# A shared expert beside a mixture's combination: four batches at a time in high and low parts, and one batch moved to it from the routing stage

## The chip, the cores and the metric

One core of one Trainium2 chip runs the whole program in one launch. The metric is the device time in microseconds (us); below it is that of the only core. The kernel before was run three times: 3481.93, 3479.44 and 3477.32 us, median 3479.44 us.

## The reference

Two decoder layers on 2048 tokens of width 512, each of self attention, cross attention and a mixture of experts, each with a residual and a layer norm. The change lies in the first layer's mixture. It has 32 routed experts of width 256 with four chosen per token and at most 80 rows each, and one shared expert of width 512 that every token passes:

```
topk_idx, topk_w = _router(x, router_w, e_bias)
...
Y = einsum('eci,eid->ecd', silu(G) * U, W_down)
out = zeros(T, d).at[slots_token].add(Yf)
shared = silu(x @ shared_gate.T) * (x @ shared_up.T) @ shared_down.T
return out + shared
```

Then `x = layernorm(x + ffn(x))`. All values are fp32.

## The kernel before

The program is written by hand as stages, each a block in which the five engines run their own instruction lists, with semaphores between them and a barrier at the end. The tokens are held as 16 batches of 128 in `moe_xall`. Three stages matter here.

*Late routing* (`late_routing`, names `cd_`). VectorE finishes the routing of the last two pairs of batches, GpSimd sends the tokens' rows to `packed`, SP loads the weights of the first eight experts (`load_first`), and TensorE fills its time with the shared expert of the first `EARLY` = 5 batches (`SharedExpert`).

*Routed experts* (`capped_experts`, `m_`). 32 experts in turn, TensorE against a ring of eight weight slots. The results go to `result` in memory. Rows of `moe_base` that hold nothing yet are borrowed as buffers.

*Combination* (`combine`, `cc_`). For every batch GpSimd gathers the four chosen rows per token (`gather`, four indirect DMAs of 256 KB, four batches ahead), VectorE adds them with their weights to `moe_base` (four L2561), takes mean and variance (L2569, L2572), GpSimd the inverse root (`norm`), and VectorE normalises into `cc_yn` (L2577), which SP stores to `x2`. Beside it the other 11 batches pass the shared expert.

`SharedExpert` works a batch at a time on unsplit fp32 operands. `turn_x` transposes the batch's tokens (L1536), ScalarE copies them out (`cc_sxT`), `up` makes the gate and the up product (L1543): for each of 4 blocks of the width, 4 products of a 128x128 weight with 128 tokens. ScalarE takes the SiLU, VectorE multiplies (`hidden`, L1525), `down` makes 4 products with 512 columns (L1564), and `add` puts the result onto `moe_base` (L1530). Each fp32 product appears in the trace as two records on TensorE. The order on TensorE is written out in `tensor`:

```
pe.wait_ge(self.act_g, done(k - 1))
self.up(pe, self.pG, self.wg, k, self.pe_g)
if k == 1:
    pe.wait_ge(self.wd_in, 16)
down(k - 1)
pe.wait_ge(self.v_h, done(k - 1))
self.up(pe, self.pU, self.wu, k, self.pe_u)
```

The shared weights lie in `all_staged`, three slots of 1 MB. When the last products have used them, ScalarE loads the next attention's three weights there (`ahead`).

## Time and profile before

| | |
|---|---|
| median of three runs | 3479.44 us |
| the profiled execution | 3482.6 us |
| its span, first to last instruction | 3480.8 us |
| mean granted TensorE clock | 0.955 |
| TensorE matmuls busy | 3159.6 us (91%) |
| VectorE busy | 2094.4 us (60%) |
| ScalarE busy | 1278.2 us (37%) |
| GpSimd busy | 1450.4 us (42%) |

The profiled execution is one execution of the same program, 3 us above the median. Busy is the time in which an engine worked on an instruction; an engine can be busy and yet not be the one that the others wait for. A row of the time line gives start, duration, engine, line, output and inputs, and in brackets how long the engine had been idle and what released it. "issue" stands where the profile shows nothing that was waited for.

### The profile page before, as it was taken

How to read it: one execution, taken by the hardware profiler on the slowest of the kernel's cores; microseconds unless marked ns; L12 is line 12 of the kernel's file. 1: busy time of each engine (PE TensorE's matmuls, PEld its weight loads, DVE VectorE, ACT ScalarE, POOL GpSimd, SP SyncE). 2: the span in 40 equal slices, each digit the busy share in tenths (PEclk: the TensorE clock that was granted, in tenths of full speed). 3: DMA queues.
4: the chain of work that ended last, by engine and by line, in shares of the span. 5: the costliest groups of instructions: out<-in, count | busy, mean ns of one | idle time of the engine just before them, and what ended most of it. 6: DMA issues, size and time to landing. Idle time of an engine off the chain costs nothing. (4 is left out here: it accounts for less than half of the span.)

```text
span 3480.8 us, 58860 instructions
## 1 busy us (share of the span) xinstructions
PE 3159.6 (91%) x21152; PEld 2638.6 (76%) x21152; DVE 2094.4 (60%) x3767; ACT 1278.2 (37%) x3276; POOL 1450.4 (42%) x1470
## 2 busy tenths in 40 slices
PE   7999999999969999799896999699999999869991
PEld 6887878878847777678685777488888888758881
DVE  5666566576645776421064777556667678645656
ACT  3333333333346666201102333244444444324430
POOL 4454343344422434300153222355555556544445
PEclk9999999999989999789998999799999999979996
DMA  4001016022310111339563112211101001156665
GB/s 172 18 16 51 0 35 232 0 95 102 141 33 24 53 32 57 144 100 340 171 143 115 37 42 63 99 56 34 36 12 47 12 24 43 39 199 223 225 221 157
DMA packets 137872, 317.18 MB, mean 91 GB/s; under 512 B 18425, under 2 KB 30457, under 8 KB 135538
## 3 DMA queue, kind: packets, MB, share of 16 engines
q1 hardware_dynamic: 120194, 274.61, 23.4%
q0 software_dynamic: 15360, 36.25, 3.9%
q10 hardware_dynamic: 2160, 4.21, 0.4%
q8 instruction: 99, 1.62, 0.2%
q14 instruction: 59, 0.48, 0.0%
HBM read 231.07 MB, written 98.04 MB: 95 GB/s over the span
## 5 line engine op out<-in xcount | busy, mean ns | idle before, releaser
L398 POOL TENSOR_TENSOR a_sq<-a_tq,a_sinq 128x256 f32<-128x256 f32 x128 | 150.3, 1194 | 358.4 <-DVE a_tq L474 358.4
L398 POOL TENSOR_TENSOR a_sk<-a_tk,a_sink 128x256 f32<-128x256 f32 x128 | 123.8, 986 | 90.0 <-DVE a_tk L474 90.0
L364 ACT COPY a_probT<-bank 128x512 f32<-128x512 f32 x64 | 37.6, 587 | 328.3 <-PE bank L713 328.3
L411 POOL TENSOR_TENSOR e_sk<-e_tk 128x512 f32<-128x512 f32 x64 | 66.6, 1040 | 204.6 <-DVE e_tk L501 204.6
L353 ACT ACTIVATE e_prob<-bank,e_nb,e_rq 128x128 f32<-128x128 f32 x256 | 113.9, 455 | 86.7 <-DVE e_nb L575 86.7
L348 ACT ACTIVATE a_sm<-a_sm,a_nmax 128x128 f32<-128x128 f32 x256 | 99.8, 391 | 121.7 <-DVE a_nmax L570 121.7
L952 ACT ACTIVATE b_prob<-bank,b_nb 128x128 f32<-128x128 f32 x512 | 139.4, 387 | 11.6 <-DVE b_nb L1148 11.3
L1046 POOL TENSOR_TENSOR d_prob<-d_prob,d_nmax 128x1024 f32<-128x1024 f32 x32 | 64.0, 1999 | 183.3 <-DVE d_nmax L1143 183.3
L2340 POOL TENSOR_TENSOR n_wu_lo<-nw_wu,n_wu_hi 128x1408 fp32r<-128x1408 f32 x23 | 74.0, 3218 | 135.4 <-DVE n_wu_hi L2384 135.4
L496 DVE TENSOR_TENSOR a_kr<-a_kr,a_sk 128x512 f32<-128x512 f32 x64 | 66.4, 1037 | 89.0 <-POOL a_sk L398 89.0
L1145 DVE TENSOR_REDUCE b_nmax<-bank 128x8 f32<-128x1024 f32 x64 | 77.9, 1217 | 68.6 <-PE bank L1289 67.9
L81 PE MATMUL bank<-a_wq_hi,a_x_lo 128*128 128x512 f32 x256 | 107.7, 421 | 7.1 <-DVE a_wq_lo L214 7.0
L943 ACT COPY b_probT<-bank 128x512 f32<-128x512 f32 x128 | 78.5, 613 | 90.5 <-PE bank L1298 90.5
L81 PE MATMUL bank<-e_wo_hi,e_z_lo 128*128 128x512 f32 x256 | 107.5, 420 | 3.1 <-DVE e_z_lo L538 3.1
L81 PE MATMUL bank<-a_wo_hi,a_z_lo 128*128 128x512 f32 x256 | 105.8, 413 | 2.9 <-DVE a_z_lo L538 2.9
L413 POOL TENSOR_TENSOR e_sq<-e_tq 128x512 f32<-128x512 f32 x64 | 66.7, 1042 | 96.3 <-DVE e_tq L505 96.3
L386 POOL TENSOR_TENSOR a_x_lo<-a_xall,a_x_hi 128x512 fp32r<-128x512 f32 x64 | 89.6, 1400 | 41.2 <-ACT a_x_hi L320 41.2
L81 PE MATMUL bank<-a_wk_hi,a_x_lo 128*128 128x512 f32 x256 | 100.7, 393 | 5.2 <-DVE a_wk_lo L214 5.1
L364 ACT COPY e_probT<-bank 128x512 f32<-128x512 f32 x64 | 37.6, 587 | 179.7 <-PE bank L713 179.7
L2345 POOL TENSOR_TENSOR n_wd_lo<-nw_wd,n_wd_hi 128x1024 fp32r<-128x1024 f32 (+1 forms) x46 | 85.8, 1885 | 39.4 <-ACT n_wd_hi L2313 39.4
L572 DVE TENSOR_REDUCE e_nmax<-bank 128x4 f32<-128x512 f32 x64 | 44.2, 690 | 96.0 <-PE bank L697 96.0
L83 PE MATMUL bank<-e_wo_hi,e_z_hi 128*128 128x512 f32 x256 | 102.0, 398 | 0.0
(512 smaller groups left out, 10718.8 us busy)
## 6 DMA issues: line engine op xcount, KB each, us to landing
packed<-all_zero SPq DMA_DIRECT2D x32, 1024.0 KB, 8.3
cw_wg<-in_c_wg SPq DMA_DIRECT2D x32, 512.0 KB
cw_wu<-in_c_wu SPq DMA_DIRECT2D x32, 512.0 KB
cw_wd<-in_c_wd SPq DMA_DIRECT2D x32, 512.0 KB
nw_wg<-in_f_wg SPq DMA_DIRECT2D x23, 704.0 KB
nw_wu<-in_f_wu SPq DMA_DIRECT2D x23, 704.0 KB
nw_wd<-in_f_wd SPq DMA_DIRECT2D x23, 512.0 KB
nw_xe<-packed SPq DMA_DIRECT2D x46, 256.0 KB, 2.7
```

Source lines behind the costliest of these rows:

```text
L81: nc.tensor.matmul(ps, a_lo, b_hi, start=start, stop=False)
L83: return nc.tensor.matmul(ps, a_hi, b_hi, start=False, stop=stop)
L348: step = nc.scalar.activation(prob[:, j, :], sm[:, j, :], ACT.Exp, bias=nmax[:, j:j + 1], accum_out=rsum[:, j:j + 1])
L353: step = nc.scalar.activation(prob[:, j, :], pS[:, P * j:P * j + P], ACT.Exp, bias=nb[:, j:j + 1], scale=rq[:, par, j:j + 1], accum_out=rs ...
L364: nc.scalar.copy(probT[:], pP[:, :]).then_inc(act_pt, 1)
L386: sub = nc.gpsimd.tensor_tensor(x_lo[:, par].rearrange("p c t -> p (c t)"), xall[:, b, :], x_hi[:, par].rearrange("p c t -> p (c t)").bitc ...
L398: step = nc.gpsimd.tensor_tensor(o, i, s, ALU.mult)
L943: nc.scalar.copy(probT[:, s // 2 % 2, s % 2], pP[:, :]).then_inc(act_pt, 1)
L952: step = nc.scalar.activation(prob[:, p % 2, i], pS[:, i // H, P * (i % H):P * (i % H) + P], ACT.Exp, bias=nb[:, p % 2, i:i + 1], scale=SCALE)
L1145: nc.vector.tensor_reduce(nmax[:, p], scores, AX.X, ALU.max, negate=True).then_inc(v_nm, 1)
L2340: nc.gpsimd.tensor_tensor(lo["u"][:, w], raw["u"][:, w], hi["u"][:, w].bitcast(F32), ALU.subtract).then_inc(g_u, 1)
L2345: sub = nc.gpsimd.tensor_tensor(o, x, y.bitcast(F32), ALU.subtract)
```

## The change

`EARLY` goes from 5 to 4, and the other 12 batches pass a new class, `SharedQuads`, in the combination: three groups of four batches. Each of the three weights and the tokens are split into a high part (a copy of type fp32r on ScalarE) and a low part (the difference, on VectorE), and each product becomes three: low by high, high by low, high by high (`split_product`, which the attentions use already). With four batches side by side a weight block stays in place for 512 columns. The hidden values are split too. Eight banks are used in pairs. The tile `cc_yn` goes, the normalised batch is written over its sum, and the gathered rows of three of the four slots go over the raw shared weights once their low parts exist. VectorE's combinations are placed by hand between the steps of a group; the last four batches have their gathered rows summed first and the shared part added last. The loads of the next attention's weights wait for the sums that read those slots.

On TensorE the start of the combination stood so (`cc_sxT` tokens, `all_staged` weights, `cc_gate` hidden values):

```order
L1536 MATMUL bank<-all_ident,moe_xall 128x128 x8
L1543 MATMUL bank<-cc_sxT,all_staged 128x128 x32
L1536 MATMUL bank<-all_ident,moe_xall 128x128 x4
L1543 MATMUL bank<-cc_sxT,all_staged 128x128 x16
L1564 MATMUL bank<-all_staged,cc_gate 128x512 x4
L1543 MATMUL bank<-cc_sxT,all_staged 128x128 x16
L1536 MATMUL bank<-all_ident,moe_xall 128x128 x4
L1543 MATMUL bank<-cc_sxT,all_staged 128x128 x16
```

Now four batches are turned first, and then every product is a triple. The first rows:

```order
L1675 MATMUL bank<-all_ident,moe_xall 128x128 x16
L81 MATMUL bank<-cc_sx_hi,cc_wg_lo 128x512
L82 MATMUL bank<-cc_sx_lo,cc_wg_hi 128x512
L83 MATMUL bank<-cc_sx_hi,cc_wg_hi 128x512
```

and the start of the down phase of the first group:

```order
L1675 MATMUL bank<-all_ident,moe_xall 128x128 x4
L81 MATMUL bank<-cc_wd_hi,cc_h_lo 128x512
L82 MATMUL bank<-cc_wd_lo,cc_h_hi 128x512
L83 MATMUL bank<-cc_wd_hi,cc_h_hi 128x512
```

Four transposes of a batch to come now stand ahead of each batch's down triples, and no down product stands between the gate and the up products.

On VectorE a batch in the middle stood so:

```order
L1525 TENSOR_TENSOR cc_gate<-cc_gate,bank 128x512
L1530 TENSOR_TENSOR moe_base<-bank,moe_xall 128x512
L2561 SCALAR_TENSOR_TENSOR cc_acc<-cc_got,moe_weight,moe_base 128x512
L2561 SCALAR_TENSOR_TENSOR cc_acc<-cc_got,moe_weight,cc_acc 128x512 x3
L2569 BN_STATS cc_stats<-cc_acc 128x6
L70 MEMSET cc_still 128x1
L2572 BN_AGGR cc_mv<-cc_stats 128x2
L2577 TENSOR_SCALAR cc_yn<-cc_acc,cc_mv,cc_rstd 128x512
```

Now, one quarter of the up phase of a group:

```order
L1661 TENSOR_TENSOR cc_gate<-cc_gate,bank 128x512
L1666 TENSOR_TENSOR cc_h_lo<-cc_gate,cc_h_hi 128x512
L2706 SCALAR_TENSOR_TENSOR cc_acc<-all_staged,moe_weight,moe_base 128x512
L2706 SCALAR_TENSOR_TENSOR cc_acc<-all_staged,moe_weight,cc_acc 128x512 x3
L2711 BN_STATS cc_stats<-cc_acc 128x6
L70 MEMSET cc_still 128x1
L2714 BN_AGGR cc_mv<-cc_stats 128x2
L2722 TENSOR_SCALAR cc_acc<-cc_acc,cc_mv,cc_rstd 128x512
```

The base add has left this place and stands in the down phase; the low part of the hidden values has come in.

The end of VectorE's list was, from the last batch's sums on:

```order
L2561 SCALAR_TENSOR_TENSOR cc_acc<-cc_got,moe_weight,moe_xall 128x512
L2561 SCALAR_TENSOR_TENSOR cc_acc<-cc_got,moe_weight,cc_acc 128x512 x3
L2567 TENSOR_TENSOR cc_acc<-bank,cc_acc 128x512
L2569 BN_STATS cc_stats<-cc_acc 128x6
L70 MEMSET cc_still 128x1
L2572 BN_AGGR cc_mv<-cc_stats 128x2
L2577 TENSOR_SCALAR cc_yn<-cc_acc,cc_mv,cc_rstd 128x512 x2
```

and the first part of the end is now:

```order
L2706 SCALAR_TENSOR_TENSOR cc_acc<-cc_got,moe_weight,moe_xall 128x512
L2706 SCALAR_TENSOR_TENSOR cc_acc<-cc_got,moe_weight,cc_acc 128x512 x3
L2706 SCALAR_TENSOR_TENSOR cc_acc<-all_staged,moe_weight,moe_xall 128x512
L2706 SCALAR_TENSOR_TENSOR cc_acc<-all_staged,moe_weight,cc_acc 128x512 x3
L1670 TENSOR_TENSOR cc_acc<-bank,cc_acc 128x512
L2711 BN_STATS cc_stats<-cc_acc 128x6
L70 MEMSET cc_still 128x1
L2714 BN_AGGR cc_mv<-cc_stats 128x2
L2722 TENSOR_SCALAR cc_acc<-cc_acc,cc_mv,cc_rstd 128x512
L2706 SCALAR_TENSOR_TENSOR cc_acc<-all_staged,moe_weight,moe_xall 128x512
L2706 SCALAR_TENSOR_TENSOR cc_acc<-all_staged,moe_weight,cc_acc 128x512 x3
L1670 TENSOR_TENSOR cc_acc<-bank,cc_acc 128x512
```

Before, one batch had its shared part added last; now the last four have, with their sums and statistics behind the last group's hidden values.

The diff, cut to its core:

```diff
+class SharedQuads:
+    QUAD = 4
...
+        self.pX, self.pG, self.pU, self.pO = (banks[:, 2 * n:2 * n + 2, :] for n in range(4))
+        self.raw, self.raw_in = [staged.tile[:, n] for n in range(3)], staged.parts
...
+    def weight_hi(self, act, n):
+        act.wait_ge(self.raw_in[n], 16)
+        self.nc.scalar.copy(self.hi[n][:], self.raw[n]).then_inc(self.w_hi[n], 1)
+    def take_x_hi(self, act, n):
+        act.wait_ge(self.pe_x, done(n))
+        if n >= self.QUAD:
+            act.wait_ge(self.pe_u, done(C * (n // self.QUAD) - 1))
+        self.nc.scalar.copy(self.x_hi[:, :, self.columns(n)], self.pX[:, n % 2].rearrange("p (c t) -> p c t", c=C)).then_inc(self.act_x, 1)
+    def scalar(self, act):
+        self.take_x_hi(act, 0)
+        self.weight_hi(act, 0)
+        for n in range(1, Q):
+            self.take_x_hi(act, n)
+        self.weight_hi(act, 1)
+        self.weight_hi(act, 2)
+        for q in range(self.quads):
+            for f in range(C):
+                k = C * q + f
+                act.wait_ge(self.pe_g, done(k))
+                act.wait_ge(self.v_hl, done(k - 2))
+                nc.scalar.activation(self.gate[:, f % 2], self.pG[:, f % 2], ACT.Silu).then_inc(self.act_g, 1)
+                act.wait_ge(self.v_h, done(k))
+                act.wait_ge(self.pe_o, done(Q * q - 1))
+                nc.scalar.copy(self.h_hi[:, f], self.h[:, f % 2]).then_inc(self.act_h, 1)
+            if q < self.quads - 1:
+                for j in range(Q):
+                    self.take_x_hi(act, Q * (q + 1) + j)
+    def weight_lo(self, dve, n):
+        dve.wait_ge(self.w_hi[n], 1)
+        self.nc.vector.tensor_tensor(self.lo[n][:], self.raw[n], self.hi[n][:].bitcast(F32), ALU.subtract).then_inc(self.w_lo[n], 1)
+    def take_x_lo(self, dve, n):
+        dve.wait_ge(self.act_x, done(n))
+        own = self.columns(n)
+        self.nc.vector.tensor_tensor(self.x_lo[:, :, own], self.pX[:, n % 2].rearrange("p (c t) -> p c t", c=C),
+                                     self.x_hi[:, :, own].bitcast(F32), ALU.subtract).then_inc(self.v_x, 1)
+    def begin_vector(self, dve):
+        self.take_x_lo(dve, 0)
+        self.weight_lo(dve, 0)
+        for n in range(1, self.QUAD):
+            self.take_x_lo(dve, n)
+        self.weight_lo(dve, 1)
+    def hidden(self, dve, k):
+        f = k % C
+        dve.wait_ge(self.act_g, done(k))
+        dve.wait_ge(self.pe_u, done(k))
+        self.nc.vector.tensor_tensor(self.h[:, f % 2], self.gate[:, f % 2], self.pU[:, f % 2], ALU.mult).then_inc(self.v_h, 1)
+    def hidden_lo(self, dve, k):
+        f = k % C
+        dve.wait_ge(self.act_h, done(k))
+        self.nc.vector.tensor_tensor(self.h_lo[:, f], self.h[:, f % 2], self.h_hi[:, f].bitcast(F32), ALU.subtract).then_inc(self.v_hl, 1)
...
+    def turn_x(self, pe, n):
+        pe.wait_ge(self.v_x, done(n - 2))
+        for c in range(C):
+            last = self.nc.tensor.transpose(self.pX[:, n % 2, P * c:P * c + P], self.xall[:, self.first + n, P * c:P * c + P], self.ident[:])
+        last.then_inc(self.pe_x, 1)
+    def up(self, ps, w, f, sem):
+        own = slice(P * f, P * f + P)
+        for c in range(C):
+            last = split_product(self.nc, ps[:, f % 2], self.hi[w][:, c, own], self.lo[w][:, c, own], self.x_hi[:, c, :], self.x_lo[:, c, :],
+                                 start=c == 0, stop=c == C - 1)
+        last.then_inc(sem, 1)
+    def down(self, pe, n):
+        q, own = n // self.QUAD, self.columns(n)
+        pe.wait_ge(self.v_b, done(n - 2))
+        for f in range(C):
+            pe.wait_ge(self.v_hl, done(C * q + f))
+            last = split_product(self.nc, self.pO[:, n % 2], self.h_hi[:, f, own], self.h_lo[:, f, own], self.hi[2][:, f, :], self.lo[2][:, f, :],
+                                 start=f == 0, stop=f == C - 1)
+        last.then_inc(self.pe_o, 1)
+    def tensor(self, pe):
+        for n in range(Q):
+            self.turn_x(pe, n)
+        for q in range(self.quads):
+            pe.wait_ge(self.v_x, done(Q * q + Q - 1))
+            for f in range(C):
+                k = C * q + f
+                if k == 0:
+                    pe.wait_ge(self.w_lo[0], 1)
+                pe.wait_ge(self.act_g, done(k - 2))
+                self.up(self.pG, 0, f, self.pe_g)
+                if k == 0:
+                    pe.wait_ge(self.w_lo[1], 1)
+                pe.wait_ge(self.v_h, done(k - 2))
+                self.up(self.pU, 1, f, self.pe_u)
+            if q == 0:
+                pe.wait_ge(self.w_lo[2], 1)
+            for j in range(Q):
+                if q < self.quads - 1:
+                    self.turn_x(pe, Q * (q + 1) + j)
+                self.down(pe, Q * q + j)
...
-        got = st.sbuf("got", [P, R, K, D])
+        own = st.sbuf("got", [P, 1 if shared else R, K, D])
-        yn = st.sbuf("yn", [P, R, D])
...
+        def got(n):
+            return own[:, n] if n == 0 or not shared else part.raw[n - 1]
...
-                for n, used in (("q", part.pe_g), ("k", part.pe_u), ("v", part.pe_o)):
-                    act.wait_ge(used, done(part.COUNT - 1))
+                for n, b in (("q", B - 3), ("k", B - 2), ("v", B - 1)):
+                    act.wait_ge(v_k, done(K * b + K - 1))
                     ahead(act, n)
...
-                sp.dma_start(x_dst[R * i + n], yn[:, n, :]).then_inc(y_out[n], 16)
+                sp.dma_start(x_dst[R * i + n], acc[:, n, :]).then_inc(y_out[n], 16)
...
-                pool.wait_ge(v_acc, done(b - R))
+                if shared and 0 < b < R:
+                    pool.wait_ge(part.w_lo[n - 1], 1)
+                if b >= R:
+                    pool.wait_ge(v_k, done(K * (b - R) + K - 1))
                 for k in range(K):
-                    nc.gpsimd.indirect_dma_start(got[:, n, k, :], None, result,
+                    nc.gpsimd.indirect_dma_start(got(n)[:, k, :], None, result,
...
+            def gathered(i, n, first):
                 b = R * i + n
                 dve.wait_ge(g_in[n], 16 * K * (i + 1))
-                dve.wait_ge(v_yn, done(b - R))
+                dve.wait_ge(y_out[n], landed(i))
                 for k in range(K):
                     if k:
-                        dve.wait_ge(v_k, done((K - 1) * b + k - 1))
-                    prev = acc[:, n] if k else part.xall[:, b] if shared_last else base[:, b]
...
+                        dve.wait_ge(v_k, done(K * b + k - 1))
+                    prev = acc[:, n] if k else first[:, b]
+                    nc.vector.scalar_tensor_tensor(out=acc[:, n], in0=got(n)[:, k, :], scalar=weight[:, b, k:k + 1], in1=prev,
+                                                   op0=ALU.mult, op1=ALU.add).then_inc(v_k, 1)
+                dve.wait_ge(v_k, done(K * b + K - 1))
+            def moments(b, n):
...
-                dve.wait_ge(y_out[n], landed(i))
-                nc.vector.tensor_scalar(yn[:, n], acc[:, n], mv[:, n, 0:1], rstd[:, n:n + 1], ALU.subtract, ALU.mult).then_inc(v_yn, 1)
+                nc.vector.tensor_scalar(acc[:, n], acc[:, n], mv[:, n, 0:1], rstd[:, n:n + 1], ALU.subtract, ALU.mult).then_inc(v_yn, 1)
+            def shared_last(b):
+                n, s = b % R, b - part.first
+                part.add(dve, s, acc[:, n], acc[:, n])
+                dve.wait_ge(part.v_b, done(s))
+                moments(b, n)
+                normed((b - 1) // R, (b - 1) % R)
             if shared:
-                head_start(dve, part.v_h, part.v_b)
+                Q, first, last = part.QUAD, part.first, part.quads - 1
+                part.begin_vector(dve)
                 b = 0
-                for k in range(part.COUNT + 1):
-                    if k < part.COUNT:
-                        part.hidden(dve, k)
-                    if 0 < k < part.COUNT:
-                        part.add(dve, k - 1)
-                    until = min(part.first + k, (k + 1) * B // part.COUNT, B)
-                    while b < until:
-                        if part.first <= b < B - 1:
-                            dve.wait_ge(part.v_b, done(b - part.first))
-                        tile(b // R, b % R, shared_last=b == B - 1)
-                        if b:
-                            normed((b - 1) // R, (b - 1) % R)
+                for q in range(part.quads):
+                    for f in range(C):
+                        part.hidden(dve, C * q + f)
+                        if q == 0 and f == 0:
+                            part.weight_lo(dve, 2)
+                        if f:
+                            part.hidden_lo(dve, C * q + f - 1)
+                        if f == C - 1:
+                            part.hidden_lo(dve, C * q + f)
+                        if b < first + Q * q:
+                            whole(b)
+                            b += 1
+                    if q < last:
+                        for j in range(Q):
+                            s = Q * q + j
+                            part.take_x_lo(dve, s + Q)
+                            part.add(dve, s, base[:, first + s, :], part.xall[:, first + s, :])
+                        dve.wait_ge(part.v_b, done(Q * q + Q - 1))
+                        whole(b)
                         b += 1
+                for c in (b, b + 1):
+                    gathered(c // R, c % R, part.xall)
+                for c in range(b, B):
+                    shared_last(c)
+                    if c + 2 < B:
+                        gathered((c + 2) // R, (c + 2) % R, part.xall)
                 normed(B // R - 1, R - 1)
                 return
...
-            EARLY = 5
-
-            def some(first, count):
-                return lambda st: SharedExpert(nc, st, psum, ident, xall, staged_c, base, first, count)
+            EARLY, QUADS = 4, 3
+            def early(st):
+                return SharedExpert(nc, st, psum, ident, xall, staged_c, base, 0, EARLY)
+            def rest(st):
+                return SharedQuads(nc, st, banks, ident, xall, staged_c, base, EARLY, QUADS)
...
                 weights = CappedWeights(Stage(nc, routed, "cw"), w)
-                late_routing(nc, "cd", psum, router, weight, some(0, EARLY), weights.load_first)
+                late_routing(nc, "cd", psum, router, weight, early, weights.load_first)
                 capped_experts(nc, psum, ident, packed1.rearrange("(e r) d -> e r d", r=80), result1, zero, weights,
                                base[0:80, B - weights.R:B], base[0:80, EARLY:EARLY + 2])
-            combine(nc, "cc", base, result1, router.rows, weight, x2, 4, some(EARLY, B - EARLY), staged_d.fetch)
+            combine(nc, "cc", base, result1, router.rows, weight, x2, 4, rest, staged_d.fetch)
```

## Rows read from the trace of the kernel before

**Rows 1.** Busy time by stage: late routing, experts, combination (engine busy us, records; TensorE clock).
```profile
1447.70:1521.60 73.90, 68.08 (x424) 56.98 (x424) 26.16 (x77) 8.23 (x15) 19.57 (x20) 0.89 0.46 172
1521.60:1717.90 196.30, 188.21 (x1280) 150.46 (x1280) 26.03 (x64) 28.36 (x64) 0.00 (x0) 0.94 0.73 246
1717.90:1864.90 147.00, 129.50 (x836) 106.47 (x836) 82.47 (x150) 11.92 (x22) 81.55 (x98) 0.93 0.65 162
```
**Rows 2.** Time line of TensorE in the combination (start us, duration us, engine, line, records).
```profile
1750.03 3.73 PE L1543 MATMUL bank<-cc_sxT,all_staged 128*128 128x128 f32 x32
...
1757.61 3.60 PE L1564 MATMUL bank<-all_staged,cc_gate 128*128 128x512 f32 x8
...
1761.05 3.73 PE L1543 MATMUL bank<-cc_sxT,all_staged 128*128 128x128 f32 x32
```
**Rows 3.** Time line of VectorE, one batch of the combination.
```profile
1764.89 0.69 DVE L1525 TENSOR_TENSOR cc_gate<-cc_gate,bank 128x512 f32<-128x512 f32 x1 [5.31 <-PE bank L1543]
1765.49 0.68 DVE L1530 TENSOR_TENSOR moe_base<-bank,moe_xall 128x512 f32<-128x512 f32 x1
1766.09 0.74 DVE L2561 SCALAR_TENSOR_TENSOR cc_acc<-cc_got,moe_weight,moe_base 128x512 f32<-128x512 f32 x1
...
1769.23 0.69 DVE L2569 BATCH_NORM_STATS2 cc_stats<-cc_acc 128x6 f32<-128x512 f32 x1
...
1770.06 0.53 DVE L2577 TENSOR_SCALAR cc_yn<-cc_acc,cc_mv,cc_rstd 128x512 f32<-128x512 f32 x1
...
1770.51 0.75 DVE L2561 SCALAR_TENSOR_TENSOR cc_acc<-cc_got,moe_weight,moe_base 128x512 f32<-128x512 f32 x1
```
**Rows 4.** Busy time by stretch, start of the combination (columns as in Rows 1).
```profile
1720.00:1726.00 6.00, 5.71 (x27) 5.74 (x28) 0.00 (x0) 0.15 (x1) 4.65 (x5) 0.50 0.68 182
1726.00:1730.00 4.00, 4.00 (x37) 4.00 (x36) 0.00 (x0) 1.07 (x2) 2.95 (x4) 0.99 0.75 215
1730.00:1742.00 12.00, 4.56 (x23) 3.42 (x22) 0.23 (x1) 0.00 (x0) 6.64 (x7) 0.76 0.65 188
```
**Rows 5.** Late routing: down products of two batches; then busy time of two stretches.
```profile
1497.81 3.67 PE L1564 MATMUL bank<-all_staged,cd_gate 128*128 128x512 f32 x8
...
1508.46 3.60 PE L1564 MATMUL bank<-all_staged,cd_gate 128*128 128x512 f32 x8
...
1450.00:1480.00 30.00, 27.07 (x168) 24.71 (x168) 9.15 (x42) 4.90 (x9) 15.39 (x16) 0.78 1.03 393
1480.00:1521.00 41.00, 38.74 (x250) 30.20 (x248) 14.53 (x26) 2.74 (x5) 2.93 (x3) 1.00 0.04 14
```
**Rows 6.** Time line, start of the next attention: copies, differences, products of parts.
```profile
1876.45 1.90 ACT L924 CAST d_wq_hi<-all_staged 128x2048 fp32r<-128x2048 f32 x1
...
1878.39 2.29 DVE L1106 TENSOR_TENSOR d_wq_lo<-all_staged,d_wq_hi 128x2048 fp32r<-128x2048 f32 x1 [1.11 <-ACT d_wq_hi L924]
...
1881.33 0.63 PE L1246 MATMUL bank<-d_wq_lo,d_x_hi 128*128 128x512 f32 x1
...
1885.59 0.63 PE L1246 MATMUL bank<-d_wq_hi,d_x_hi 128*128 128x512 f32 x1
...
1886.95 0.39 PE L1246 MATMUL bank<-d_wk_hi,d_x_lo 128*128 128x512 f32 x1
...
1889.44 0.39 PE L1246 MATMUL bank<-d_wv_hi,d_x_hi 128*128 128x512 f32 x1
```
**Rows 7.** Time line of GpSimd in the combination, gathers.
```profile
1771.87 1.04 POOL L2532 DMA_INDIRECT cc_got<-result,moe_rows  x1 [0.18 <-issue]
1773.22 1.23 POOL L2532 DMA_INDIRECT cc_got<-result,moe_rows  x1 [0.30 <-issue]
...
1778.14 0.99 POOL L2532 DMA_INDIRECT cc_got<-result,moe_rows  x1 [0.18 <-issue]
...
1832.43 1.33 POOL L2532 DMA_INDIRECT cc_got<-result,moe_rows  x1 [0.30 <-issue]
```
**Rows 8.** Time line of VectorE, last instruction of the combination.
```profile
1864.34 0.55 DVE L2577 TENSOR_SCALAR cc_yn<-cc_acc,cc_mv,cc_rstd 128x512 f32<-128x512 f32 x1 [0.71 <-POOL cc_rstd L2540]
```

More of the change, by code:

```diff
@@ L2500, in _ @@
             def _(pe):
-                part.begin(pe)
                 part.tensor(pe)
@@ L2550, in _ @@
         def _(dve):
[L2551 to L2553 removed]
+            head_start(dve, v_k, v_st, v_mv, v_yn)
+            def gathered(i, n, first):
                 b = R * i + n
                 dve.wait_ge(g_in[n], 16 * K * (i + 1))
[L2556 removed]
+                dve.wait_ge(y_out[n], landed(i))
                 for k in range(K):
                     if k:
[L2559 to L2568 removed]
+                        dve.wait_ge(v_k, done(K * b + k - 1))
[4 more added lines that the diff above has]
+            def moments(b, n):
                 nc.vector.bn_stats(stats[:, n], acc[:, n]).then_inc(v_st, 1)
```

42 lines of the change are left out of this document (31 added, 11 removed).

## The prediction, before the changed kernel was run

> **What bounds the kernel now.** I read the page's totals and slices first, then the busy time by stage, then the time line inside the two stages that the change touches. The page names VectorE and GpSimd at the very end, but no step of the edit lies there. [Rows 1] cut out the three stages that matter: end of routing with five shared batches (73.9 us), routed experts (196.3 us), combination with eleven shared batches (147.0 us). In all three TensorE is busy for nine tenths, so I look for the period of one batch on TensorE. [Rows 2]: in the combination a gate product starts at 1750.03 and the next one at 1761.05, so a shared batch costs 11.02 us. It consists of 4 transposes, 64 records of 128 columns (about 7.1 us) and 8 records of 512 columns (1757.61 to 1761.05, 3.4 us). VectorE's batch beside it is in [rows 3]: hidden product and base add take 0.60 us each from start to start (1764.89, 1765.49, 1766.09), the combination of one batch 4.42 us (1766.09 to 1770.51): the four weighted sums 3.14 us, statistics and mean/variance 0.83 us, normalising 0.45 us. VectorE therefore waits for TensorE now.
>
> One thing is odd. [Rows 4]: from 1720 to 1726 the clock is at half (1.2 GHz), then full, and from 1730 to 1742 TensorE starts only 23 records in 12 us with the DMA engines at 0.65. Those records should have taken 23 x 0.11 = 2.5 us, so some 9.5 us are lost there, while sixteen gathers run back to back. Later gathers ([rows 7]) run beside matmuls at full pace, so this belongs to the start of the stage.
>
> **The late routing stage: one batch less (5 to 4).** [Rows 5]: the down products of two successive batches start at 1497.81 and 1508.46, 10.65 us apart. The batch removed is one without anything new in its place. What could hide it is the first load of the eight experts' weights on SP: the DMA engines are full until 1480 (1.03) and nearly idle from 1480 to 1521 (0.04). So nothing that the experts wait for lands late, and the stage ends 10.65 us earlier. The experts behind it are TensorE's (188.2 of 196.3 us busy, [rows 1]) and only shift. The two rows of the base buffer that they borrow move from batches 5 and 6 to 4 and 5, at no cost. Term: **-10.65 us**.
>
> **The combination: twelve batches in three groups of four.** I lay the new order out from the stage's start at 1718.0, with 0.1 us from one engine's end to another's start (a choice).
>
> Products. A batch had 32 + 4 fp32 products; a group of four now has 96 up and 48 down, every one 512 columns wide, fp32r. [Rows 6] have the same triple in the next attention: eleven starts from 1886.95 to 1889.44 give 0.2264 us each at full clock, ten from 1881.33 to 1885.59 give 0.426 us at half clock. A group costs 144 x 0.2267 = 32.6 us and 16 transposes at 0.11 us, 1.8 us: 34.4 us, 8.6 us a batch against 11.02.
>
> Head, new. Weights and tokens have to be split before the first product. First transposes as now, token copy 0.6 us, weight copy on ScalarE 1.90 us, weight difference on VectorE 2.29 us [rows 6], then three token differences at 0.6 us behind it in VectorE's queue. The fourth transpose waits for the second difference, since two banks are used. First product at 1726.7, against 1721.2 now: 8.7 us from the stage's start.
>
> Group 0, up: 96 products, the first 14 at half clock (6 us, as in [rows 4] and [rows 6]), the others at 0.2267: 24.9 us, to 1751.6. The other two weight differences (2.3 us each) end before their product needs them. Down: 12.6 us, and two waits. VectorE has hidden, low part and a combination at each quarter, 0.61 + 0.61 + 4.43 = 5.65 us, against TensorE's 24 x 0.2267 = 5.44 us; it starts with the extra weight difference, so the first down product waits 1.7 us for the low part of h. The third batch's transpose waits 1.2 us for a token difference that stands behind a combination. 15.8 us, to 1767.4.
>
> Group 1: 21.8 up, 12.6 down, 0.5 of the same waits: 34.9 us, to 1802.3. Group 2, up: 21.8 us, to 1824.1.
>
> Tail, new and the largest loss. VectorE holds its last four batches here: hidden work until about 1826.6; two batches of weighted sums 6.2 us; then four times add, statistics, normalising (0.61 + 0.86 + 0.46 = 1.93, 7.7 us); two more batches of sums 6.2 us; the last batch's root on GpSimd and its normalising, 1.6 us. End at 1848.3. Down products 3 and 4 wait 3.5 and 2.3 us for the adds that free their banks, and don't decide.
>
> GpSimd: four gathers and a root take 6.27 us (1771.87 to 1778.14, [rows 7]). Against combinations 5.65 us apart it falls behind inside a group and catches up in the down phase; in my schedule no VectorE row waits for it until then. The gathers of batches 1 to 3 now wait for a weight difference each, since they overwrite the raw weights. The third comes at 1738.3 and is needed at 1755. The next attention's three weight loads, which waited for TensorE's last products, now wait for sums that end 6 to 15 us before the stage's end, about as now. Stores go from the sum's own buffer; batch 15's sum waits for the store of batch 11, 5 us earlier.
>
> Now the last normalising starts at 1864.34 and lasts 0.55 us [rows 8]: 146.9 us from 1718.0. New: 8.7 + 24.9 + 15.8 + 34.9 + 21.8 + 24.2 = 130.3 us. That is -16.6 us, of which the odd gap of 9.5 us is more than half. I give back 1 us for the half clock that two waits in the tail may bring: **-15.6 us**.
>
> **Sum.** -10.65 - 15.6 = -26.3 us. The profiled execution took 3482.6 us (span 3480.8): 3456.3. The median of the runs is 3479.4: **3453 us**.
>
> **Bounds of what no row shows.** Products at 0.235 instead of 0.2267: +1.5. Weighted sums at 0.75 or 0.85 each instead of 0.78: -1.3 or +3.2. Head without any half clock: -2.3. Stores landing 7 us after issue instead of 5: +2. The low part of h reads two SBUF operands; taken as 0.61, since the weighted sum with two such operands takes 0.75. These make 3448 to 3459 around the forecast.
>
> **A rule of the skill against it.** [Rows 7] show the same gather at 1.04 and 1.23 us, the longer one while VectorE sums. The Trainium skill (GPSIMD Engine Reference, Key points) says that GpSimd shares its SBUF interfaces with VectorE and that VectorE instructions with two SBUF inputs contend with it. By that rule, which the rows bear out, the change has VectorE in such instructions more densely and gathers get dearer. It is the second rival below.
>
> **The rivals.**
> 1. *The slow start comes back.* The gap of [rows 4] begins after some 75 matmuls of the stage. Such a place would come in group 0, in the third gate product. For it: the gathers still run from the start and the program still jumps there. Against it: gathers are now broken by waits for weight differences, and TensorE uses up instructions at half the rate. Laid out with 10 us lost there, the stage ends at 1857.3 instead of 1848.3: 3462 us.
> 2. *GpSimd sets the pace.* Every gather at the longest of [rows 7], 1.33 us, and 0.30 us to the next makes, with a root of 1.2 us, 7.7 us a batch, and VectorE waits for roots and rows within each group. Laid out: +3.9 us, 3457 us.
> 3. *The batch taken from routing was hidden*, behind the sends or the weight load: then only the combination counts, 3464 us. Against it the DMA share of 0.04 in [rows 5].
> 4. *Slower: the clock stays at 1.2 GHz in the combination.* TensorE and VectorE now hand over in small steps, and [rows 4] have the clock fall from 0.99 to 0.76 on average while starts are sparse. If every product costs 0.426 us, the stage ends at 1917.5 us, 69 us later than laid out: 3522 us. It decides from 26.3 / 0.199 = 132 of the 432 products on. Against it: up phases are 96 products without a wait, and the same triple runs at 0.2264 in [rows 6]. The Trainium skill (TensorE: Matmul & The Clock Gate, What's actually happening) has the array throttled by default and released by activity. By that rule the waits between the phases could throttle it again, which is this rival; the half clock at 1720 to 1726 agrees with it.
>
> **Chances.** Forecast 0.55, rival 1 0.25, rival 2 0.10, rival 3 0.06, rival 4 0.04. About 0.2% (7 us) is what a measurement of this kernel can tell from no change. Forecast and rivals 1 to 3 are each more than that below 3479.4; only two or three of them together come within it. So faster 0.94, within 0.03, slower 0.03. The range takes in the forecast's own bounds and rival 1 with its bounds up to 3466: 3447 to 3466.
>
> **What would show it.** Right: first product some 8.7 us into the stage; 0.227 us between products after 6 us; three groups of about 40, 35 and 46 us; VectorE with almost no idle time in the last 22 us; late routing 10.7 us shorter; experts unchanged. Wrong: "issue" as releaser on TensorE in group 0 (rival 1), VectorE waiting for a root or a gather inside an up phase (rival 2), experts longer than 196.3 us (rival 3), clock under 0.9 in group 1 (rival 4). A next attention whose first weight copy starts more than 12.1 us after the last normalising (1876.45 in [rows 6], 1864.34 in [rows 8]) would show that its loads now come too late, which I count at nothing.

## The result, and the profile after

| | before | after |
|---|---|---|
| median, runs beside each other | 3480.68 us (4 runs) | 3455.87 us (4 runs) |
| ratio, 95% interval | | 0.9928 [0.9911, 0.9944] |
| the same once more, later | 3481.58 us (9 runs) | 3457.69 us (5 runs), 0.9930 [0.9917, 0.9944] |
| profiled execution / span | 3482.6 / 3480.8 us | 3457.2 / 3455.4 us |
| mean granted TensorE clock | 0.955 | 0.954 |

Faster by 0.7%: 24.8 us, and 23.9 us the second time; forecast were 26.3 us and 3453 us. First the busy time by stage after the change: late routing, experts, then the combination cut at its own joints (head, group 0 up, group 0 down, group 1, group 2 up, tail). The columns are those of [rows 1]: start:end and length, then TensorE products, weight loads, VectorE, ScalarE and GpSimd busy, the clock, DMA share, GB/s.

```profile
1448.90:1513.10 64.20, 57.30 (x348) 48.08 (x348) 24.86 (x75) 7.16 (x13) 19.52 (x20) 0.88 0.53 198
1513.10:1707.10 194.00, 186.71 (x1280) 149.59 (x1280) 26.02 (x64) 28.30 (x64) 0.00 (x0) 0.96 0.74 249
1707.10:1716.60 9.50, 4.17 (x16) 3.00 (x16) 4.87 (x5) 4.71 (x6) 7.29 (x8) 0.50 0.41 117
1716.60:1741.00 24.40, 24.39 (x101) 20.05 (x102) 18.46 (x26) 7.08 (x9) 18.69 (x18) 0.92 0.53 159
1741.00:1757.00 16.00, 13.70 (x65) 10.40 (x64) 12.50 (x24) 2.87 (x5) 12.73 (x17) 1.00 0.83 187
1757.00:1791.50 34.50, 34.39 (x159) 28.00 (x158) 27.15 (x48) 7.12 (x12) 22.93 (x26) 1.00 0.94 183
1791.50:1813.30 21.80, 21.80 (x98) 18.06 (x97) 20.38 (x35) 4.26 (x7) 13.90 (x16) 1.00 0.54 139
1813.30:1841.90 28.60, 13.42 (x48) 9.47 (x47) 22.79 (x44) 0.62 (x1) 12.49 (x17) 0.79 0.85 223
```

The stages are 64.2, 194.0 and 134.8 us long, against 73.9, 196.3 and 147.0 in [rows 1] (cut there at slightly other places; the table below has the same cut for all). TensorE fills group 1 and the up phase of group 2: 34.39 of 34.50 us and 21.80 of 21.80, at clock 1.00. It does not fill the tail: 13.42 of 28.60. VectorE should fill that, and has 22.79.

What it waits for there, as the sum of VectorE's waits from 1813.3 to 1842 after the change (us in total, times, longest):

```profile
DVE cc_acc L2706 <- DMA x<-cc_acc: 4.1, 1, 4.1
DVE cc_acc L2722 <- POOL cc_rstd L2684: 0.7, 1, 0.7
```

And on the time lines of VectorE, of ScalarE's queue and of SP's, of the same execution:

```profile
1828.82 0.52 DVE L2722 TENSOR_SCALAR cc_acc<-cc_acc,cc_mv,cc_rstd 128x512 f32<-128x512 f32 x1
...
1833.42 0.75 DVE L2706 SCALAR_TENSOR_TENSOR cc_acc<-all_staged,moe_weight,moe_xall 128x512 f32<-128x512 f32 x1 [4.08 <-DMA x<-cc_acc]
...
1841.33 0.55 DVE L2722 TENSOR_SCALAR cc_acc<-cc_acc,cc_mv,cc_rstd 128x512 f32<-128x512 f32 x1 [0.71 <-POOL cc_rstd L2684]
```
```profile
1822.14 0.34 ACTq L1489 DMA_DIRECT2D all_staged<-in_d_wq  x1
1827.27 0.33 ACTq L1489 DMA_DIRECT2D all_staged<-in_d_wk  x1
1836.57 0.33 ACTq L1489 DMA_DIRECT2D all_staged<-in_d_wv  x1
```
```profile
1824.38 17.85 SPq L2652 DMA_DIRECT2D x<-cc_acc  x5
```

Batch 15's sum needs the place in which batch 11 lies. That store is the first of the five in the last row, asked for at 1824.4, right after batch 11 is normalised, and the sum starts at 1833.4, 4.1 us after it could have, so the store took some 9 us to free its place. Ahead of it, at 1822.1, the next attention's first weights were asked for, 1 MB, and 1 MB more at 1827.3.

The stages in all traces, cut at the same five instructions (first load of late routing's expert weights; first load of the experts' rows; first instruction of the combination, on GpSimd; the first of the two instructions of its last root; the next attention's first weight copy, which is `d_wq_hi` in [rows 6]). These are differences of start times, in us:

| kernel | start | late routing | experts | combination | root to copy | rest | span |
|---|---|---|---|---|---|---|---|
| before | 1447.7 | 74.7 | 195.6 | 145.3 | 13.2 | 1604.3 | 3480.8 |
| the change | 1448.9 | 64.2 | 194.0 | 133.2 | 13.1 | 1602.0 | 3455.4 |
| the change, again | 1446.7 | 64.4 | 194.0 | 132.9 | 13.2 | 1600.2 | 3451.4 |
| batch moved only | 1443.4 | 64.0 | 194.4 | 155.6 | 13.0 | 1602.8 | 3473.2 |
| unsplit | 1451.4 | 63.8 | 194.1 | 144.7 | 12.9 | 1598.6 | 3465.5 |
| gathers spaced | 1442.3 | 74.5 | 194.2 | 141.8 | 13.0 | 1607.7 | 3473.5 |
| gathers one batch at a time | 1448.3 | 74.7 | 194.0 | 132.6 | 13.1 | 1599.9 | 3462.6 |
| loads late | 1443.1 | 63.9 | 194.4 | 129.2 | 15.9 | 1604.6 | 3451.1 |
| own place | 1445.0 | 64.0 | 194.0 | 130.0 | 13.4 | 1603.8 | 3450.2 |
| batch 8 earlier | 1451.0 | 64.1 | 194.2 | 126.0 | 13.0 | 1603.7 | 3452.0 |
| both | 1448.1 | 64.0 | 194.1 | 125.5 | 13.1 | 1603.6 | 3448.4 |
| both, again | 1449.5 | 64.1 | 194.2 | 125.8 | 13.1 | 1606.3 | 3453.0 |
| twelve gathers | 1448.1 | 64.1 | 194.0 | 130.8 | 13.0 | 1606.4 | 3456.4 |

What no edit touches, everything ahead of the start and behind the copy, varies by 9 us each between executions. For the same code the combination repeats to 0.3 us and late routing to 0.6 us. So the stages are read from this table, and the times below only say whether they add up. The experts' 195.6 us belongs to that one execution: each other trace has 194.0 to 194.4, with five batches in routing as with four.

### The profile page after: what moved, and what is told of

Its sections match the earlier page's. It is cut to its first block and busy times, and to the rows that moved or that the text cites. A ratio compares the mean times of both kernels' runs of the same rounds, so it can differ in the third digit from the quotient of the medians.

```text
span 3455.4 us, 58053 instructions
## 1 busy us (share of the span) xinstructions
PE 3126.9 (90%) x20720; PEld 2609.3 (76%) x20720; DVE 2117.7 (61%) x3794; ACT 1291.1 (37%) x3291; POOL 1456.0 (42%) x1470
## 5 line engine op out<-in xcount | busy, mean ns | idle before, releaser
L952 ACT ACTIVATE b_prob<-bank,b_nb 128x128 f32<-128x128 f32 x512 | 139.1, 386 | 13.6 <-DVE b_nb L1148 13.4
L1046 POOL TENSOR_TENSOR d_prob<-d_prob,d_nmax 128x1024 f32<-128x1024 f32 x32 | 63.9, 1998 | 181.5 <-DVE d_nmax L1143 181.5
```

Source lines behind the costliest of these rows:

```text
L952: step = nc.scalar.activation(prob[:, p % 2, i], pS[:, i // H, P * (i % H):P * (i % H) + P], ACT.Exp, bias=nb[:, p % 2, i:i + 1], scale=SCALE)
```

## Experiments

**The moved batch by itself.** The kernel before, one batch less in routing and twelve in the combination.

```diff
-            EARLY = 5
+            EARLY = 4
```

> The kernel before with one batch moved and nothing else: 4 batches by the routing, 12 in the combination, all by the old products. If a shared batch costs what it did in either place: late routing 10.6 us shorter, combination 11.0 us longer, sum +0.4 us, that is no difference to the kernel before (ratio 0.999 to 1.001). Rival: the combination had room beside its gathers, so that a twelfth batch is partly hidden there and moving alone gains 5 to 10 us (ratio 0.997 to 0.9985).

3479.96 us against 3480.96, ratio 1.0000 [0.9991, 1.0009]. Late routing is 10.7 us shorter, the combination 10.3 us longer. The move alone earns nothing. It also refutes rival 3: the batch in routing was not hidden.

**Wide and stationary, but not split.** The change with its groups of four and its order, every product on fp32 operands, no high or low part. Two things go with it: the raw weights stay in use, so all four batches of gathered rows have buffers of their own and their gathers wait for no weight difference; and the next attention's loads wait for TensorE's last products again, not for sums.

```diff
-            last = split_product(self.nc, ps[:, f % 2], self.hi[w][:, c, own], self.lo[w][:, c, own], self.x_hi[:, c, :], self.x_lo[:, c, :],
-                                 start=c == 0, stop=c == C - 1)
+            last = self.nc.tensor.matmul(ps[:, f % 2], self.raw[w][:, c, own], self.x_hi[:, c, :], start=c == 0, stop=c == C - 1)
...
```

> The changed kernel with four batches at a time and weights in place for 512 columns, but unsplit fp32 products (48 per group instead of 144) and no copies or differences of weights, tokens and hidden values. If the gain comes from the high and low parts: a product of 512 columns takes 0.86 us against 0.68 us for a triple, 22.7 us more in products, 4.5 us less in the head and about 3 us less waiting, so some 15 us slower than the changed kernel, near 3471 us. Rival: the wide products with weights in place carry the gain: within 3 us of the changed kernel, 3453 to 3459 us.

3470.70 us, ratio 0.9969 [0.9957, 0.9981]. The combination is 144.7 us, 10.9 less than with the batch moved only and 11.5 more than the change. The first step is not the wider product: four records of 128 columns take 4 x 0.111 = 0.44 us [rows 2], one of 512 columns 3.4 / 8 = 0.43 us. What has gone is the slow start. GpSimd's sixteen gathers still follow on one another, nearly all every 1.25 us, and in the stretch where the kernel before starved TensorE is busy (busy time from 1712 to 1736, without splitting):

```profile
1712.00:1736.00 24.00, 23.27 (x53) 10.62 (x52) 4.48 (x8) 3.33 (x6) 18.53 (x21) 0.85 0.69 194
```

**The slow start in the kernel before.** Its first gathers are held until TensorE has got somewhere. First spacing: batch 1 behind the gate products of batch 0, batch 2 behind its up products, batch 3 behind batch 1's gate products.

```diff
+                if shared and 0 < b < R:
+                    used, k = ((part.pe_g, 0), (part.pe_u, 0), (part.pe_g, 1))[b - 1]
+                    pool.wait_ge(used, done(k))
```

> The kernel before, with the gathers of batches 1, 2 and 3 each held back until TensorE has finished a further product of the first two shared batches. If the slow stretch at the start (23 records in 12 us, 9.5 us lost) comes from sixteen gathers issued without a pause, it goes: records at full pace between 1730 and 1742, ratio about 0.997. Rival: the slow stretch belongs to TensorE's own instruction supply after the stage's jump and stays, with or without gathers: ratio 0.999 to 1.001.

3477.96 us, ratio 0.9986 [0.9977, 0.9995]. The stretch did not go, it moved. The time line of TensorE, kernel before (first fence) and with this spacing (second):

```profile
1730.90 0.38 PE L1536 MATMUL bank<-all_ident,moe_xall 128*128 128x128 f32 x2
...
1733.03 0.27 PE L1536 MATMUL bank<-all_ident,moe_xall 128*128 128x128 f32 x1 [1.13 <-issue]
...
1735.86 0.40 PE L1543 MATMUL bank<-cc_sxT,all_staged 128*128 128x128 f32 x2 [1.14 <-issue]
...
1740.11 0.37 PE L1543 MATMUL bank<-cc_sxT,all_staged 128*128 128x128 f32 x1 [0.63 <-issue]
```
```profile
1734.61 0.94 PE L1543 MATMUL bank<-cc_sxT,all_staged 128*128 128x128 f32 x7
1736.99 0.39 PE L1543 MATMUL bank<-cc_sxT,all_staged 128*128 128x128 f32 x2 [1.44 <-issue]
...
1743.35 2.52 PE L1543 MATMUL bank<-cc_sxT,all_staged 128*128 128x128 f32 x11 [0.82 <-issue]
```

Before, sixteen gathers run unbroken from 1718.8; starts become sparse with the tenth (1730.2), and the stretch ends some 4 us after the last (1737.7). With this spacing 12 follow on one another from 1720.5 to 1735.0, the sparse starts begin at the twelfth, and end 2.5 us after the last gather of the next batch (1740.9). The place in TensorE's program is another one, the place in the row of gathers nearly the same. The run with only the batch moved shows the stretch too, again from the tenth gather on and until 3.7 us after the last. So the spacing was made wider:

```diff
-                    used, k = ((part.pe_g, 0), (part.pe_u, 0), (part.pe_g, 1))[b - 1]
+                    used, k = ((part.pe_g, 0), (part.pe_g, 1), (part.pe_g, 2))[b - 1]
```

> The kernel before with the gathers of batches 1, 2, 3 held until the gate products of batches 0, 1, 2 have begun to be done, so that no more than 4 to 8 follow on one another at the start. In the first spacing 12 followed on one another and the slow stretch only moved, from the 10th of a row of 16 gathers to the 12th of 12, and ended some 3 us behind the last one each time. Theory (a long unbroken row of gathers starves TensorE's instructions of 128 columns): no waits on issue over 2 us in all, the combination (145.3 us from its first instruction to its last root) 8 to 9.5 us shorter, about 136 to 137, the time about 3472. Rival (the stretch belongs to the program's first batches, however the gathers lie): waits on issue of 5 us or more, again at the second or third batch, time 3478 or more. Second rival (gathers that come later make VectorE late, which gives back what TensorE gains): no issue waits, but the combination at 141 us or more.

3471.18 us against 3481.66, ratio 0.9967 [0.9955, 0.9979]. No wait on issue is left, and TensorE is busy from end to end (12 us and 6 us from 1729.3 on):

```profile
1729.30:1741.30 12.00, 12.00 (x87) 10.09 (x86) 5.47 (x10) 1.07 (x2) 5.52 (x6) 1.00 0.53 152
1741.30:1747.30 6.00, 6.00 (x33) 4.15 (x33) 3.96 (x8) 0.00 (x0) 1.89 (x2) 1.00 0.10 29
```

The combination takes 132.6 us instead of 145.3. The stretch cost 12.7 us, not 9.5: behind it the kernel before also had six microseconds at a clock of 0.62:

```profile
1742.00:1748.00 6.00, 6.00 (x27) 5.28 (x27) 4.25 (x8) 0.00 (x0) 1.21 (x3) 0.62 0.00 0
```

Three waits alone, without the change, give two fifths of what the change gives.

**Twelve gathers at once in the changed kernel.** Meant to bring the unbroken row back: the gathers of batches 1 and 2 go to free rows of `moe_base` and no longer wait for the weight differences.

```diff
+        def place(b):
+            return base[:, 4 * b + 4:4 * b + 8] if shared and isinstance(b, int) and b in (1, 2) else got(b % R)
...
```

> The changed kernel with the gathers of batches 1 and 2 sent to rows of the shared expert's output that are free until group 1, so that twelve gathers or more are issued back to back from the stage's start as in the kernel before, and not behind the copies of the weights. The slow stretch of the kernel before (TensorE at 23 records in 12 us, waits put down to issue) moved from 1730 to 1742 to 1736 to 1748 when its first gathers were spaced out. Theory (the stretch needs gathers and products of 128 columns together: with four batches unsplit, 512 columns wide, it was gone although the gathers moved 200 GB/s): no issue waits on TensorE, time within 2 us of the change's, 3454 to 3458. Rival 1 of the prediction (the burst alone brings the slow start back): issue waits of 5 us or more on TensorE in group 0, time about 3462.

3458.22 us, ratio 0.9932 [0.9917, 0.9946], no issue waits on TensorE. This run tells less than it was made for. The change already issues twelve gathers unbroken, from 1707.9 to 1725.8, so the edit altered nothing at the start; what kept them apart there was VectorE (last section). The run without splitting is the better evidence.

**The weight loads later.** All three of the next attention's loads wait for batch 15's sum.

```diff
-                for n, b in (("q", B - 3), ("k", B - 2), ("v", B - 1)):
+                for n, b in (("q", B - 1), ("k", B - 1), ("v", B - 1)):
```

> The changed kernel, with the three weight loads of the next attention all held back until the last batch's sum has been read. If batch 15's sum waited 4.1 us for batch 11's store because that store ran behind the 1 MB load issued 2 us before it: the wait shrinks to under 1 us, the combination ends 3 to 4 us earlier, and the next attention starts as soon as before, since its weights are needed 12 us after the stage's last normalising. Rival: the store is late from the gathers alone, and the wait stays at 3 to 4 us; or the three loads in a row arrive too late, and the next attention's first weight copy starts up to 5 us later.

3453.41 us, ratio 0.9926 [0.9913, 0.9940]: in time no difference from the change. The stages say why. VectorE's wait on the store is gone (no row of it is left), the combination is 4.0 us shorter, and the next attention's first weight copy comes 2.8 us later behind the last root (15.9 against 13.1). It fits that the loads, asked for at 1826.9 to 1827.8, then stand in front of batch 15's store and the read of `x2`, as they had stood in front of batch 11's store; this was not tested by itself. 1.2 us stay.

**A place of its own for batch 15's sum.** It no longer waits for batch 11's store; the loads stay where they were.

```diff
-        acc = st.sbuf("acc", [P, R, D])
+        acc = st.sbuf("acc", [P, R + 1 if shared else R, D])
+
+        def at(i, n):
+            return R if shared and isinstance(i, int) and R * i + n == B - 1 else n
...
```

> The changed kernel with a fifth place for the sums, used by batch 15 alone, so that its sum need not wait until batch 11 is stored. Theory (the 4.1 us for which VectorE waited on that store are the tail's missing term, and nothing stands behind them): the wait is gone, the last normalising ends some 4 us earlier in the stage (about 130.7 us instead of 134.8), the next attention starts 12 us behind it as before, and the time is about 3452. Rival (what the tail saves is given back in the start of the next attention, as when the weight loads came later: 2.7 of 3.9 us): stage 4 us shorter, gap to the first weight copy 14 to 15 us, time about 3455. Second rival (the store was only a cover for TensorE or the gathers): VectorE waits at the same place for something else, nothing moves.

3456.19 us, ratio 0.9936 [0.9922, 0.9950]. As a time this is no difference. In the stages the combination is 3.2 us shorter and root to copy 0.3 us longer; of the 4.1 us, 1.1 came back as a wait for the batch's gathered rows:

```profile
DVE cc_acc L2711 <- DMA all_staged<-result,moe_rows: 1.1, 1, 1.1
```

**Work moved out of the tail.** In group 1's down phase VectorE was busy 6.55 of 12.5 us:

```profile
1779.00:1791.50 12.50, 12.39 (x60) 9.76 (x59) 6.55 (x10) 2.87 (x5) 6.29 (x8) 1.00 0.95 175
```

Batch 8 is combined there in four pieces, the batches behind it move up.

```diff
+                            if q == last - 1:
+                                i, n = b // R, b % R
+                                if j == 0:
+                                    dve.wait_ge(part.v_b, done(s))
+                                    gathered(i, n, base, range(0, 2))
+                                elif j == 1:
+                                    gathered(i, n, base, range(2, 4))
...
```

> The changed kernel with another order on VectorE: batch 8 is combined in four pieces inside the down phase of group 1, batch 9 at its end, 10 and 11 and the first sums of 12 and 13 inside the up phase of group 2. VectorE stood idle there for about 6 of 12.5 us and works the whole tail. Theory (the tail is VectorE's work): one batch and two sums less in the tail, some 6 us, of which the store of batch 11 takes back up to 2 us since it is asked for earlier too but batch 15 reaches it sooner: time about 3451. Rival (TensorE's group 2, not VectorE, sets the tail): stage shorter by under 1 us, time 3455 to 3456. Second rival (VectorE's pieces delay the low parts of h in group 1, so TensorE waits there): waits over 2 us on TensorE in group 1 or at group 2's down phase.

3453.80 us, ratio 0.9919 [0.9906, 0.9933]; combination 126.0, 7.2 us shorter. The wait on the store falls to 0.4 us by itself:

```profile
DVE cc_acc L2706 <- DMA x<-cc_acc: 0.4, 1, 0.4
```

VectorE's work between batch 11's normalising and batch 15's sum is the same as in the change, 5.6 us. It is the store that frees its place sooner, 5.4 us after it was asked for instead of 9.0, although the first weight load goes out 2.2 us ahead of it here too. What differs is the gathers: the last one was issued 4.2 us ahead of the store, in the change 1.9 us. What the DMA engines moved from the store's issue until the sum could start (the gathered rows are all that were still to come):

| version | of the weight loads | gathered rows | store's issue to start |
|---|---|---|---|
| the change | 2.10 MB | 0.52 MB | 9.0 us |
| the change, again | 1.98 MB | 0.64 MB | 8.8 us |
| twelve gathers | 1.48 MB | 0.49 MB | 6.6 us |
| batch 8 earlier | 1.25 MB | 0.12 MB | 5.4 us |
| loads late | none | 0.51 MB | at most 4.9 us (VectorE did not wait) |

So the load alone does not make the nine microseconds: with few gathered rows left the store took 5.4 us behind it, and with rows left but no load at most 4.9. The traces with both lie between 6.6 and 9.0 us, and that spread is not explained. No run changed the gathers alone, so their part is read off these traces and not tested.

**Both.**

> Both edits together: fifth place for batch 15's sum and batch 8 inside group 1. Theory (the two terms are apart from each other): the stage is about 10 us shorter than the change's 134.8, the gap to the next attention's first weight copy stays near 12 us, time about 3446. Rival (the end of the stage meets TensorE's last products or the loads of the next attention's weights): stage 4 to 6 us shorter or gap 15 us, time 3450 to 3452.

3451.04 us, ratio 0.9915 [0.9902, 0.9929]; combination 125.5. The two terms are not apart, as I had put it (I expected about 3446 us): the first edit's wait was nearly gone with the second. The last two stretches of this version, group 2 up and the tail:

```profile
1790.00:1811.40 21.40, 21.40 (x96) 17.70 (x96) 19.84 (x35) 4.26 (x7) 17.51 (x18) 1.00 0.72 191
1811.40:1833.30 21.90, 12.95 (x53) 9.24 (x51) 19.35 (x37) 0.62 (x1) 9.19 (x12) 0.90 0.90 247
```

The tail is 21.9 us instead of 28.6, VectorE works 19.35 of it.

**The change and the best version once more, beside each other.**

> The changed kernel once more, unedited, beside the next run on the same chip. The wait of batch 15's sum on the store of batch 11 was 4.1 us in its first trace and 1.7 us in the trace of twelve gathers at once, whose rows after the start are the same otherwise. If the wait belongs to the order of the work, it is 3.5 us or more again; if it is the landing that varies, it comes out anywhere between 0 and 4 us, the stage with it, and my term for the tail was short by less than 4.1 us in most executions. Time 3454 to 3458, experts 194.0 us, late routing 64.1 us, as in the other traces.

> Both edits together once more, to set them against the change on one chip. Theory: the stage is 7 to 8 us shorter than the change's, the time 5 to 8 us below it, near 3449. Rival: the first comparison, 3451.0 against medians of the change between 3454 and 3458, was the spread of the stages outside, and the two agree within 2 us.

3457.69 and 3452.30 us (ratios 0.9930 [0.9917, 0.9944] and 0.9913 [0.9899, 0.9926]). The wait on the store was 3.9 us in the change's second trace, so it came back for the same code; the 1.7 us of the twelve gathers is not explained. The best version was below the change in both comparisons, by 4.8 and 5.4 us, and its combination by 7.7 and 7.1 us. The intervals of the ratios still touch, so the times alone would not carry it; times and stages together do.

## Why the prediction was right, and which terms were not

**Late routing, one batch less.** Right: -10.5 us against -10.65. The period read off two down products [rows 5] was the price.

**The combination.** -15.6 us forecast, -12.1 found (146.9 to 134.8). By the steps of the layout:

| step | forecast | found |
|---|---|---|
| head | 8.7 | 9.5 |
| group 0, up | 24.9 | 24.4 |
| group 0, down | 15.8 | 16.0 |
| group 1 | 34.9 | 34.5 |
| group 2, up | 21.8 | 21.8 |
| tail | 24.2 | 28.6 |

Product pace and groups were right within half a microsecond; the product pace from [rows 6] held. Two of my sums do not come out of their own terms: group 0 up adds up to 24.6 us, not 24.9, and its down phase to 15.5, not 15.8. In group 0 I counted the half clock too long: the time line of TensorE has ten products before the pace goes from 0.426 to 0.227 us, not fourteen, while the first product came 0.8 us later, behind the token differences.

**The step that was mis-sized is the tail's store.** "Batch 15's sum waits for the store of batch 11, 5 us earlier" took its landing as 5 us, and the bound as 7; it took 9. The first of the three weight loads, which I had placed "about as now", goes out 2.2 us ahead of the store, and 0.52 MB of gathered rows are still to come. The late loads show that the wait needs the loads: with them out of the way it is gone. They do not make it alone: after batch 8's move the store took 5.4 us behind the same load. The wait cost 4.1 us of the 4.4 by which the tail was short. The 1 us given back for the clock bought nothing: some eight products did run at half pace behind TensorE's wait of 3.2 us, but VectorE waited for none of them. The sign that I had named for loads that come too late did not show: the next weight copy starts 12.05 us after the last normalising, as before (12.1).

**The sum.** Late routing and combination together gave 22.6 us in the traces where 26.3 were forecast; the times gave 24.8 and 23.9, with intervals of about 5 to 6 us either side. No stage that the edit touches explains why the times gave 1 to 2 us more than the stages; that lies within what the untouched stages vary. So it is in part luck that the forecast median, 3453 us, lies within 3 us of the measured one.

**Rival 1, the slow start.** It did not come: no issue waits on TensorE in the combination, whose group 0 took the forecast time. Half of my reason against it was wrong: I counted on the weight copies breaking the row of gathers, and twelve ran unbroken. The other half, fewer instructions per time, agrees with the run without splitting, where sixteen gathers at 1.25 us left TensorE busy. My price of the stretch, 9.5 us, left out the half clock behind it (12.7 measured).

**Rival 2, GpSimd.** TensorE never waited in group 1 or in group 2's up phase, and VectorE never for a gathered row, and for a root only at the very end, 0.7 us. The gathers did get dearer, most of all at the start (2.5 us, last section), but nobody waited for them.

**Rival 3** fell with the moved batch (ratio 1.0000). **Rival 4:** the clock was 1.00 from 1741 to 1813, and 0.79 in the tail, where VectorE decides.

**Where the 12 us in the combination come from**, in the order of the table: 145.3 before; without the slow stretch 132.6; one batch more, at 11.0 [rows 2], 143.6 (worked out, not run); wide and unsplit 144.7; split, 133.2. The high and low parts are worth 11.5 us, net of what comes with them (copies and differences, and the 4.1 us on the store, which the unsplit run does not have); the move in routing is worth 10.5, and the batch that it brings into the combination takes 11.0 back. What is left of the gain, 12.7 less the 1.1 of the wide form, is the slow stretch, which both wide forms remove. The two middle steps are differences between versions, not edits made one on the other.

## What to carry to other kernels

When a kernel loses time in a stretch that the profile puts down to issue, move what runs beside it before rewriting the stage: three waits gave 10.5 us here. When a change shifts the bound from TensorE to VectorE at a stage's end, follow each store whose place is used again, and look at what goes out in front of it, on any queue: with 1 MB ahead and gathered rows still to come a store took 6.6 to 9.0 us here, without the load at most 4.9. Where the untouched stages vary by more than the effect, cut the traces at the same instructions and compare stage lengths, and let the medians only confirm them.

## What the runs showed of the hardware

**A long row of gathers can starve TensorE.** With products of 128 columns, TensorE began work only every 0.7 to 1.4 us, one or two records at a time for the most part, from the tenth to twelfth unbroken gather on, until 2.5 to 4 us after the last. With 512 columns a row of sixteen did nothing, and with 128 columns and rows of four neither. What in the chip does this was not tried; the DMA share alone is not enough, since TensorE ran full beside 0.94 in group 1.

**Gathers stretch beside VectorE.** The time line of GpSimd and that of VectorE at the change's start:

```profile
1710.49 0.95 POOL L2676 DMA_INDIRECT cc_got<-result,moe_rows  x1 [0.30 <-issue]
1711.74 2.51 POOL L2676 DMA_INDIRECT cc_got<-result,moe_rows  x1 [0.30 <-issue]
...
1717.05 0.95 POOL L2676 DMA_INDIRECT all_staged<-result,moe_rows  x1 [0.30 <-issue]
1718.31 2.46 POOL L2676 DMA_INDIRECT all_staged<-result,moe_rows  x1 [0.30 <-issue]
```
```profile
1711.14 2.29 DVE L1641 TENSOR_TENSOR cc_wg_lo<-all_staged,cc_wg_hi 128x2048 fp32r<-128x2048 f32 x1 [1.11 <-issue]
...
1717.66 2.29 DVE L1641 TENSOR_TENSOR cc_wu_lo<-all_staged,cc_wu_hi 128x2048 fp32r<-128x2048 f32 x1 [1.11 <-ACT cc_wu_hi L1609]
```

Both gathers issued inside a weight difference of 2.29 us last until 0.8 us after its end, 2.5 us instead of 0.95. The difference itself keeps its 2.29 us, as in the next attention [rows 6], where no gather runs. The Trainium skill (GPSIMD Engine Reference, Key points) says that VectorE instructions with two SBUF inputs contend with GpSimd; both inputs are in SBUF here, and the rows agree. The loss is GpSimd's alone, and about 1.5 us a time.
